# Moving the read-out products of a recurrent layer to GpSimd, and one power in place of a square root, a reciprocal and a Newton step

## What is computed

```
r = (xr @ Wr.T).reshape(B, L, H, S)        # H = 32 heads of S = 8 channels
k = (xk @ Wk.T).reshape(B, L, H, S)
v = (xv @ Wv.T).reshape(B, L, H, S)
g = jax.nn.silu(xg @ Wg.T)
def step(s, inp):
    k_l, v_l, w_l, r_l = inp
    a = k_l[..., :, None] * v_l[..., None, :]
    out = jnp.einsum('bhs,bhst->bht', r_l, faaaa * a + s)
    s_new = a + w_l[..., None] * s
    return (s_new, out)
_, outs = jax.lax.scan(step, s0, seq)
y = outs.transpose(1, 0, 2, 3)
gm = jnp.mean(y, axis=-1, keepdims=True)
gv = jnp.mean((y - gm) ** 2, axis=-1, keepdims=True)
y = ((y - gm) * jax.lax.rsqrt(gv + EPS)).reshape(B, L, C) * gn_w + gn_b
x = x + y * g @ Wo.T
```

## Time and profile before

| | |
|---|---|
| median of 3 runs | 1333.27 us (1333.21 to 1338.27) |
| the profiled execution's own time | 1336.37 us |
| its span, first to last instruction | 1334.6 us |
| PE busy | 1229.8 us (92%) |
| DVE busy | 807.0 us (60%) |
| ACT busy | 536.7 us (40%) |
| POOL busy | 180.2 us (13%) |
| the recurrent stage | from 197.3 to 482 us of the span |

### The profile page before, as it was taken

How to read it: one execution, slowest core, us unless ns; L and a number is a source line. 1 busy time by engine, 2 the same in 40 slices (tenths; PEclk the granted TensorE clock), 3 DMA queues, 4 the chain that set the end, 5 groups by cost and what they waited for, 6 DMA issues and landing times.

```text
span 1334.6 us, 17906 instructions
## 1 busy us (share of the span) xinstructions
PE 1229.8 (92%) x6056; PEld 862.5 (65%) x6064; DVE 807.0 (60%) x2386; ACT 536.7 (40%) x1233; POOL 180.2 (13%) x397
## 2 busy tenths in 40 slices
PE   7769788898989787999999699999999999999999
PEld 4347555464555343444443488888888888888887
DVE  4434337586958336787785466666666666666620
ACT  3235343343534324555455343344343434334432
POOL 3122013022212111102011100000000000000000
PEclk9779899899989879999999899999999999999999
DMA  7454623101111535543524733030303030500000
GB/s 224 129 146 127 199 74 117 71 32 64 40 56 49 151 134 153 175 130 118 170 77 140 255 130 119 9 127 0 127 0 127 0 127 0 190 1 1 1 9 24
DMA packets 100652, 127.59 MB, mean 96 GB/s; under 512 B 6737, under 2 KB 78577, under 8 KB 98321
## 3 DMA queue, kind: packets, MB, share of 16 engines
q1 hardware_dynamic: 99936, 126.14, 29.1%
q10 hardware_dynamic: 624, 0.30, 0.1%
HBM read 79.33 MB, written 46.79 MB: 95 GB/s over the span
## 4 chain that ended last, share of the span: by engine, by line
PE 77%; DMA 8%; DVE 5%; ACT 3%; SPq 2%; issue 2%; POOL 2%; ACTq 0%; POOLq 0%; DVEq 0%
PE J L2448 8%; PE J L2466 8%; PE TT L2456 8%; PE S L2422 4%; PE OO L1077 4%; PE TT L2432 4%; PE OO L2422 4%; PE OO L1074 3%; PE J L324 2%; PE J L1077 2%; PE J L1343 2%; PE OO L2666 2%; PE S L634 2%; DMA km<-query_parts 2%; PE J L1074 2%
## 5 line engine op out<-in xcount | busy, mean ns | idle before, releaser
L2524 ACT ACTIVATE PT<-TT 128x512 f32<-128x512 f32 x128 | 76.5, 597 | 281.2 <-PE TT L2432 281.2
L2595 DVE TENSOR_SCALAR QK<-J,cols 128x256 f32<-128x256 f32 x126 | 61.0, 484 | 69.6 <-PE J L2448 69.6
L2559 POOL COPY On<-probs 128x8 f32<-128x8 f32 x128 | 29.1, 227 | 475.3 <-DVE probs L2584 446.0
L2584 DVE TENSOR_SCALAR probs<-probs,inv 128x257 f32<-128x257 f32 x256 | 79.1, 352 | 4.5
L1077 PE MATMUL OO<-ctxT,weights_a 128*128 128x512 f32 x136 | 69.9, 638 | 12.3 <-SPq L308 9.5
L2432 PE MATMUL TT<-ident,probs 128*128 128x128 f32 x512 | 76.9, 273 | 1.7 <-DVE probs L2584 1.7
L1074 PE MATMUL OO<-weights_a,ctxT 128*128 128x512 f32 x136 | 67.8, 622 | 9.8 <-SPq L308 6.1
L2432 PEld LDWEIGHTS TT<-ident,probs 128*128 128x128 f32 x512 | 63.8, 141 | 15.7 <-DVE probs L2584 3.0
L2590 DVE COPY km<-TT 128x256 f32<-128x256 f32 x128 | 54.2, 423 | 31.0 <-PE TT L2456 30.8
L970 DVE CUSTOM_DVE_ANT_0 mask_b<-S,weights_a 128x256 f32<-128x256 f32 x64 | 24.6, 422 | 70.0 <-PE S L634 69.8
L2576 DVE TENSOR_REDUCE maxes<-S 128x1 f32<-128x257 f32 x128 | 48.4, 420 | 30.4 <-PE S L2422 30.4
(11 more groups left out here) (413 smaller groups left out, 2704.4 us busy)
## 6 DMA issues: line engine op xcount, KB each, us to landing
wide_keys<-weights_a SPq DMA_DIRECT2D x64, 256.0 KB, 2.1
wide_values<-weights_a SPq DMA_DIRECT2D x56, 256.0 KB, 2.0
query_parts<-weights_a SPq DMA_DIRECT2D x48, 192.0 KB, 2.8
weights_a<-wide_keys SPq DMA_DIRECT2D x16, 512.0 KB, 7.2
weights_a<-wide_values SPq DMA_DIRECT2D x16, 512.0 KB, 8.4
early<-wide_keys SPq DMA_DIRECT2D x16, 512.0 KB, 8.2
early<-wide_values SPq DMA_DIRECT2D x16, 512.0 KB, 8.7
weights_a<-key_parts SPq DMA_DIRECT2D x16, 288.0 KB
```

The source lines that it names most:

```text
L2524: act.activation(PT[:, n % 2, :], T0[:, :], ACT.Copy).then_inc(pt3_ready, 1)
L2584: ins = dve.tensor_scalar(P_[n % 2][:, qt, :], P_[n % 2][:, qt, :], inv[:, qt, n % 32:n % 32 + 1], None, ALU.mult)
L2595: dve.tensor_scalar(QK[:, n % 2, 0, 0:S], J0[:, 0:S], head_cols(f"bq{a + 1}")[:, h:h + 1], float(DIM3) ** -0.5, ALU.add, ALU.mult).then_in ...
```

## The change

The eight products of state and receptance leave DVE and are issued by POOL, one after each state. POOL's two gate products now stand after the products of j = 2 and j = 3, bonus times v after that of j = 5, and all else of POOL after the eighth product and the power. The root on ACT, the reciprocal and the Newton step on DVE go; POOL computes variance to the power of -0.5, 128x64, in one instruction, which DVE's next product waits for. The tail of the sequence before, and in sequence 3 the splitting of keys and queries, stand behind that power on POOL.

```diff
                     late(0)
-                    act.wait_ge(gvar_ready, 1)
-                    act.activation(root, var, ACT.Sqrt).then_inc(groot_ready, 1)
                     late(1)
...
-                    pool.wait_ge(g_ready, 1)
-                    pool.tensor_tensor(gated_w, silu_g, row("L1_xattn_gn_w").unsqueeze(1).to_broadcast([P, TQ, C]),
-                                       ALU.mult)
-                    pool.tensor_tensor(gated_b, silu_g, row("L1_xattn_gn_b").unsqueeze(1).to_broadcast([P, TQ, C]),
-                                       ALU.mult).then_inc(gates_ready, 1)
-                    pool.wait_ge(v_ready, 1)
-                    pool.wait_ge(bonus_ready, 1)
-                    pool.tensor_tensor(tmp3, v_tok[:, :, :].rearrange("p t (h j) -> p (t h) j", j=DIM1),
-                                       bonus.unsqueeze(2).to_broadcast([P, TQ * HEADS1, DIM1]), ALU.mult)\
-                        .then_inc(bonus_times_v, 1)
+                    pool.wait_ge(r_ready, 1)
+                    for j in range(DIM1):
+                        pool.wait_ge(state_ready, j + 1)
+                        if j >= 4:
+                            pool.wait_ge(y_done, (j - 4) // 2 + 1)
+                        pool.tensor_tensor(read[j % 4], rT, state[j % 2][:, :, 0:S], ALU.mult).then_inc(read_ready, 1)
+                        if j == 2:
+                            pool.wait_ge(g_ready, 1)
+                            pool.tensor_tensor(gated_w, silu_g, row("L1_xattn_gn_w").unsqueeze(1).to_broadcast([P, TQ, C]),
+                                               ALU.mult)
+                        if j == 3:
+                            pool.tensor_tensor(gated_b, silu_g, row("L1_xattn_gn_b").unsqueeze(1).to_broadcast([P, TQ, C]),
+                                               ALU.mult).then_inc(gates_ready, 1)
+                        if j == 5:
+                            pool.wait_ge(v_ready, 1)
+                            pool.wait_ge(bonus_ready, 1)
+                            pool.tensor_tensor(tmp3, v_tok[:, :, :].rearrange("p t (h j) -> p (t h) j", j=DIM1),
+                                               bonus.unsqueeze(2).to_broadcast([P, TQ * HEADS1, DIM1]), ALU.mult)\
+                                .then_inc(bonus_times_v, 1)
+                    pool.wait_ge(gvar_ready, 1)
+                    pool.tensor_tensor(root, var, halves[:, 0:1].to_broadcast([P, TQ * HEADS1]), ALU.pow)\
+                        .then_inc(groot_ready, 1)
                     if b_before is not None:
                         finish_tail(b_before, 1)
...
-                        dve.wait_ge(state_ready, j + 1)
-                        if j >= 4:
-                            dve.wait_ge(y_done, (j - 4) // 2 + 1)
-                        dve.tensor_tensor(read[j % 4], rT, state[j % 2][:, :, 0:S], ALU.mult).then_inc(read_ready, 1)
...
                     dve.wait_ge(groot_ready, 1)
-                    chain.link(dve.reciprocal(root, root))
-
-                    chain.link(dve.tensor_tensor(mean, root, root, ALU.mult))
-                    chain.link(dve.tensor_tensor(mean, mean, var, ALU.mult))
-                    chain.link(dve.tensor_scalar(mean, mean, -0.5, 1.5, ALU.mult, ALU.add))
-                    chain.link(dve.tensor_tensor(root, root, mean, ALU.mult))
```

## The result

The changed kernel takes 1377.03 us (median of 4 runs, 1375.86 to 1380.72) against 1335.77 us of the kernel before in the same session: a ratio of 1.0317, with a 95% interval of 1.029 to 1.0344. All ratios leave out one slow execution, of 1627.9 us at a granted clock of 0.74, of the kernel with the gate weight on POOL.

A forecast was written before the change was run, and what follows sets the result against it. The prediction took TensorE to bound the scan, and DVE's group norm chain, or in sequence 3 a line of transfers, the sequence ends. Its terms added 66.5 us to 1333.3, giving 1399.8, named as 1399 us; range 1350 to 1410.

The forecast's parts named there:

- The scan is TensorE's; the products that move cost nothing: Scan rounds: TensorE needs 4.7 us each, DVE's stay 2.3 to 2.5 us, so moving products costs and gains nothing.
- ACT's tables cost nothing: Before the scan in sequences 1 to 3: a 1.3 us table load absorbed by DVE's idle time; other bound 3.9 us.
- The root goes, 1.91 us: Between variance and first wide product at each sequence's end: the old root's 1.91 us disappears.
- The power, 16.4 us: POOL's 64-column power in each sequence: 253 ns a column plus 190 ns, 16.4 us; paid by column given 0.52.
- something between: Rival for the power's length: 4 to 12 us, adding 17 to 49 us, 1350 to 1382 us; chance 0.28.
- The collision with the tail, 1.9 us in sequences 1 and 2: After the power, the tail's two POOL products meet DVE's wide instructions, lengthening DVE's chain by 1.9 us.
- The splits behind the power in sequence 3: Key and query splits wait for variance, power and tail, so SP's query stores start 18.9 us later.
- T: Length in us of POOL's 64-column power, in the forecast's added time of 3.7 + 4 x (T - 0.7).
- The sum: Added time: 14.6 us in sequence 0, 16.5 each in 1 and 2, 18.9 in 3, together 66.5 us.
- The cheap power: Rival: the power's 506 ns are paid once, 0.7 to 1.4 us long, 1337 to 1340 us; under 4 us given 0.15.
- The faster case: Rival: DVE bounds the scan, so moved products save 19.2 us; 1318 us with a cheap power; chance 0.05.
- The clock: After longer pauses, a second slow stretch of TensorE costs some 2 us a sequence, 8 us at most.

The follow-up runs named there:

- the kernel with the gate weight on POOL: Centred read-out times gate weight moved to POOL, against the kernel with products on POOL and ahead units dealt 14, 14, 14, 14; 1323.19 us, ratio 0.9921.
- the products alone: Changed kernel with root, reciprocal and Newton step put back, so only the eight products a sequence move to POOL; 1329.77 us, ratio 0.9993.
- The exchange of power and tail: Changed kernel with POOL's power moved behind the tail and, in sequence 3, behind the splits; 1362.57 us, ratio 1.023.
- The width series: Kernel before plus eight powers of 1 to 64 columns and a plain product in POOL's idle time at the end; 1335.35 us, single run.

## Why the prediction held, and where it was off

- *The scan is TensorE's; the products that move cost nothing.* Right, but the room was less than I said. With the products alone the ratio is 0.9993, and doubling them shows that the cover is there and how thin it is. My 4.7 us of TensorE a round was misread: the stretch to 313.70 holds more than the eight rounds, whose last gather starts at 305.39. The gathers of two rounds stood 7.22 us apart, 3.6 a round against DVE's 2.48:

```profile
292.56 0.64 PE L1937 MATMUL OO<-km,head 128*32 128x256 f32 x8
299.78 0.64 PE L1937 MATMUL OO<-early,head 128*32 128x256 f32 x8
```

  I had put it at nothing gained; 1.5 us are gained in sequence 0, where TensorE did wait for a product. I had read the waits of sequence 1 only.
- *ACT's tables cost nothing.* The traces bear it out within some 0.2 us. The first scan starts 22.7 us into sequence 1, against 23.9 before, and 23.6 us into sequence 2, against 22.7. The clock after the meetings accounts for 1.4 us less and 0.8 us more (below). No run tested it by itself.
- *The root goes, 1.91 us.* Right: with a power of 0.70 us and a product of 0.29 us in its place, sequence 0 is 0.9 us shorter.
- *The power, 16.4 us.* This term was mis-sized: it measured 10.53 us. The time came out in the case of something between, to which I had given 0.28, and not in the one that I took and gave 0.52; the range held because it spanned both. The mechanism was right, a power is paid by the column, but I gave the instruction a fixed part of 190 ns from plain instructions and put the whole rest of the two-column power, 506 ns, on two columns: 253 ns each. The width series shows 0.35 us once and 159 ns a column. An error of 94 ns a column, times 62, is the 5.9 us. One short shape can't separate the two parts, and the text had said so of a loop whose first result is late.
- *The collision with the tail, 1.9 us in sequences 1 and 2.* Right in size: DVE's instructions took 1.74 + 1.63 in place of 2 x 0.69 us, 1.99 us more. The exchange of power and tail gave back 0.9 us in sequence 1, or 2.0 with the clock's 1.1 us added back, and 2.1 in sequence 2.
- *The splits behind the power in sequence 3.* Right: with T = 10.53 the prediction's terms give 18.9 - 5.9 = 13.0 us, and SP's query stores start 13.0 us later in the sequence. In the profiles sequence 3 grew by 11.7 us, 1.3 less, because its twelve matmuls took 7.12 us and not 8.39 at the clocks granted. Some 9 us went when the power stood behind tail and splits, 1.3 of them by the clock.
- *The sum.* 3.7 + 4 x (10.53 - 0.7) = 43.0 us, against 42.3 us by the ratio (0.0317 x 1335.77) and 39.8 us by the profiles' sequences. With the right length of one instruction the prediction would have said 1376 us. That it is so close to 1377.03 is in part luck: the formula leaves out the 1.5 us that the products gain, while the kernel before had a median of 1335.77 us beside the changed one and not the 1333.3 that I built on, and the two nearly cancel.
- *The rivals.* The cheap power, at 1337 to 1340 us, was built and gave 1.0064, about 1342 us on 1333.3, near but above what I had for 1.0 us: its own formula gives 3.7 + 1.2 = 4.9 us, the runs 8.5 (4.7 to 12.4). Its profile has 4.1 us of lower clock in it, against that of the products alone; whether its other runs had the same, no trace shows. The faster case is excluded: the products' move gains 1.5 us in the profiles and not 19.2, and doubling them costs sequences 1 and 2 only some 3 us each.
- *The clock.* I had allowed for 8 us more by longer pauses. After the longer pauses the slow stretch was no longer. These are the first 8 us after the meetings that end sequence 1 (pause of 15.4 us) and sequence 0 (13.4 us):

```profile
331.60:335.60 4.00, 3.91 (x6) 1.75 (x7) 2.87 (x9) 0.10 (x1) 1.38 (x2) 0.50 0.02 4
335.60:339.60 4.00, 4.00 (x18) 2.80 (x17) 0.52 (x2) 1.82 (x4) 0.00 (x0) 0.86 0.19 66
258.40:262.40 4.00, 3.93 (x9) 1.97 (x10) 2.90 (x9) 0.36 (x1) 1.36 (x2) 0.60 0.02 6
262.40:266.40 4.00, 4.00 (x19) 2.76 (x18) 0.64 (x3) 1.37 (x4) 0.00 (x0) 1.00 0.17 66
```

  Before, after pauses of 4.7 us, it was 0.57 and 1.00 in the place of the first two and 0.50 and 0.75 in that of the last two. So nothing was added over the stage, but the clock moved time between the sequences. By an estimate from these rows (8 us times the difference of the mean clocks), sequence 1 lost 1.4 us less to slow matmuls than before, and sequence 2 0.8 us more. By the table they grew by 9.3 and 11.5 us; with the clock taken out both grew by 10.7, where the prediction's terms give 10.6.
- The Trainium skill's GPSIMD Engine Reference (Performance versus the Vector engine), which gives a two-input instruction 2.6 cycles an element and no figure for a power, would have led to +2 us. The plain product of 64 columns took 0.29 us, where that figure on the 0.19 us of fixed cost gives 0.33, an estimate: near. The power of the same width is 36 times as long, and the measurement decides.

## What to carry to other kernels

An instruction that stands on the path to a meeting is worth its length once for every meeting, and what is queued behind it on its engine comes on top; on an engine with an in-order queue, put the work that others wait for ahead of the one that waits. Price an operation that the trace shows only in a small shape by a series of widths, before a large one is put on the path. A pause of TensorE at a meeting is room for work that must be done anyway, and here closing it to 1.5 us also kept the clock at full speed. When profiles of two kernels are compared stretch by stretch, compare the granted clock of the stretches first: here it made differences of 1 to 2.5 us that the edits themselves don't account for.

## What the runs showed of the hardware

- A POOL power of 128 partitions by n columns takes 0.35 us and 0.159 us a column (n from 16 to 64), a plain product of 64 columns 0.29 us.
- At a meeting TensorE was granted half speed after a pause of 4.7 us and full speed after one of 1.5 us; the half-speed stretch after a pause of 15.4 us was no longer than after 4.7 us (0.50 and 0.86 over twice 4 us, against 0.50 and 0.75).
- Two scans on DVE (inputs in SBUF) that met a POOL product with both inputs in SBUF took 1.84 to 1.91 us in place of 1.39. They grew by 0.5 us and not by the product's 1.18: the product had started 0.46 and 0.53 us ahead of them, beside DVE's product with one input in PSUM. That one took 0.66 us beside POOL's, and 0.67 us without it. In the timeline of sequence 1 after the change:

```profile
281.29 1.39 DVE L2323 TENSOR_TENSOR_SCAN early<-km,early 128x256 f32<-128x256 f32 x2
...
283.29 1.91 DVE L2323 TENSOR_TENSOR_SCAN early<-km,early 128x256 f32<-128x256 f32 x2
285.13 0.66 DVE L2306 TENSOR_TENSOR early<-km,TT 128x512 f32<-128x512 f32 x1
285.82 1.84 DVE L2323 TENSOR_TENSOR_SCAN early<-km,early 128x256 f32<-128x256 f32 x2
...
282.83 1.19 POOL L2195 TENSOR_TENSOR early<-km,early 128x512 f32<-128x512 f32 x1 [5.99 <-DVE early L2323]
```
